# Iterated attention: the Newton step of the layer norm on GpSimd, another VectorE order, and another division of the last sums

## The reference

```python
def step(carry, _):
    q_cur, converged = carry
    scores = jnp.einsum('bhqd,bhkd->bhqk', q_cur, k) / scale
    attn = jax.nn.softmax(scores, axis=-1)
    out = jnp.einsum('bhqk,bhkd->bhqd', attn, v)
    diff = jnp.linalg.norm(out - q_cur)
    q_new = jnp.where(converged, q_cur, out)
    return ((q_new, converged | (diff < UPDATE_STEPS_EPS)), None)
(q_final, _), _ = jax.lax.scan(step, (q, jnp.asarray(False)), None, length=UPDATE_STEPS_MAX)
merged = q_final.transpose(0, 2, 1, 3).reshape(x.shape[0], x.shape[1], INNER)
return merged @ Wo + bo
```

## Time and profile before

| | before |
|---|---|
| median of 3 runs | 3225.08 us (3224.71 to 3231.12) |
| profiled execution, its own time | 3228.11 us |
| its span | 3226.8 us |
| PE busy in the span | 2926.5 us (91%) |
| DVE, ACT, POOL busy | 2524.8, 2207.4, 2008.9 us |
| mean granted clock of TensorE | 0.966 |
| iterated attention | from about 1635 us to the end |

### The profile page before, as it was taken

The page is one execution under the profiler, slowest core; times in us unless marked ns, Lnnn a source line. Parts: engine busy times, 40 slices in busy tenths (PEclk is TensorE's granted clock), DMA queues, the critical chain, the costliest instruction groups (busy, mean ns, idle before and its releaser), DMA issues.

```text
span 3226.8 us, 72034 instructions
## 1 busy us (share of the span) xinstructions
PE 2926.5 (91%) x24662; PEld 2238.6 (69%) x24663; DVE 2524.8 (78%) x5836; ACT 2207.4 (68%) x6152; POOL 2008.9 (62%) x2045
## 2 busy tenths in 40 slices
PE   5999888897799989999979999999999999999997
PEld 4666554465688868787867777777777777777775
DVE  6788887757777765564568888888888888888886
ACT  4566655653355556456448888888888888888885
POOL 2633333232455555335148888888888888888884
PEclk7999989998899989999989999999999999999998
DMA  3222422100000010201000000000000000000000
GB/s 110 74 77 77 128 78 76 52 1 7 1 1 1 1 50 24 63 1 50 14 14 2 2 2 2 2 2 2 2 2 2 2 2 2 1 2 2 1 2 27
DMA packets 68872, 77.15 MB, mean 24 GB/s; under 512 B 8017, under 2 KB 60321, under 8 KB 68385
## 3 DMA queue, kind: packets, MB, share of 16 engines
q1 hardware_dynamic: 64912, 71.10, 7.2%
q10 hardware_dynamic: 3600, 1.46, 0.2%
HBM read 52.61 MB, written 18.87 MB: 22 GB/s over the span
## 4 chain that ended last, share of the span: by engine, by line
PE 38%; DVE 9%; POOL 8%; issue 5%; ACT 4%; DVEq 0%; POOLq 0%; ACTq 0%
PE psum L2556 9%; PE psum L2538 7%; PE psum L2520 6%; POOL attn_p L3018 4%; DVE attn_pt L2817 2%; DVE sb_few L2804 2%; PE psum L1902 2%; PE psum L1753 2%; ACT attn_p L2662 2%; PE psum L1995 2%; PE psum L1755 2%; PE psum L1754 2%; PE psum L2583 2%; PE psum L1802 2%; PE psum L2462 1%
## 5 line engine op out<-in xcount | busy, mean ns | idle before, releaser
L3018 POOL TENSOR_TENSOR attn_p<-attn_p,sb_few 128x512 f32<-128x512 f32 x768 | 796.0, 1050 | 174.8 <-DVE sb_few L2811 173.5
L2662 ACT ACTIVATE attn_p<-psum,sb_few 128x256 f32<-128x256 f32 x1536 | 720.2, 479 | 61.4 <-DVE sb_few L2804 61.3
L2804 DVE TENSOR_REDUCE sb_few<-psum 128x2 f32<-128x512 f32 x768 | 507.9, 679 | 12.7 <-PE psum L2520 7.0
L2538 PE MATMUL psum<-sb_kept,attn_p 128*128 128x128 f32 x3072 | 411.4, 277 | 33.2 <-DVE attn_pt L2817 29.4
L2556 PE MATMUL psum<-attn_pt,attn_v 128*64 128x256 f32 x3072 | 384.2, 387 | 30.7 <-DVE attn_pt L2817 30.7
L502 DVE TENSOR_REDUCE sb_a_nm<-psum 128x2 f32<-128x512 f32 x512 | 329.0, 684 | 87.5 <-PE psum L392 54.1
L2538 PEld LDWEIGHTS psum<-sb_kept,attn_p 128*128 128x128 f32 x3072 | 335.4, 141 | 82.5 <-issue 30.7
L568 ACT ACTIVATE sb_a_pt<-psum 128x512 f32<-128x512 f32 x512 | 278.5, 597 | 100.4 <-PE psum L399 69.7
L2662 ACT ACTIVATION_READ_ACCUMULATOR attn_p<-psum,sb_few 128x1 f32 x1536 | 319.6, 208 | 0.0
L2556 PEld LDWEIGHTS psum<-attn_pt,attn_v 128*64 128x64 f32 x3072 | 202.7, 136 | 157.0 <-issue 75.5
L2817 DVE COPY attn_pt<-psum 128x512 f32<-128x512 f32 x384 | 263.7, 687 | 34.0 <-PE psum L2538 28.7
(11 more groups left out here) (441 smaller groups left out, 7752.1 us busy)
## 6 DMA issues: line engine op xcount, KB each, us to landing
sb_a_spread<-a_spilled SPq DMA_DIRECT2D x64, 256.0 KB, 2.9
a_spilled<-sb_a_part_hi SPq DMA_DIRECT2D x64, 128.0 KB
a_spilled<-sb_a_part_lo SPq DMA_DIRECT2D x64, 128.0 KB
sb_a_spread<-a_spilled SPq DMA_DIRECT2D x64, 128.0 KB, 2.7
sb_gate_up<-in_L_ffn_Wg SPq DMA_DIRECT2D x32, 128.0 KB
sb_gate_up<-in_L_ffn_Wu SPq DMA_DIRECT2D x32, 128.0 KB
sb_down_w<-in_L_ffn_Wd SPq DMA_DIRECT2D x32, 128.0 KB, 2.5
sb_x<-in_L_attn_x SPq DMA_DIRECT2D x4, 512.0 KB, 7.3
```

The source lines that it names most:

```text
L2538: mm = pe.transpose(PT(e)[:, kt * N + t * P:kt * N + (t + 1) * P], Pr[p % 3][:, e, t, kt * P:(kt + 1) * P], c.ident)
L2662: ins = act.activation(Pr[p % 3][:, e, t, :], S(p, e)[:, t * N:(t + 1) * N], ACT.Exp, bias=nm[:, p % 4, e, t:t + 1], accum_out=rsum[:, p % ...
L2804: dve.tensor_reduce(nm[:, p % 4, e, :], S(p, e).rearrange("p (t n) -> p t n", t=TB), AX.X, ALU.max, negate=True).then_inc(maxed.sem, 1)
L3018: pool.tensor_tensor(P3, P3, spread(rinv[:, p % 4, e, :], N), ALU.mult).then_inc(normed[e].sem, 1)
```

## The change

It does the following.

- The Newton step of every unit but the first moves from DVE to POOL, in four operations (r*r, v*that, -0.5*that+1.5, r*that), each waiting for the one before. It stands behind the first norm of rounds 3 and 4. The first unit's stays on DVE (`newton_first`).
- DVE's order: `variance(u+1, 0)` goes from the end of round 2 to behind the first maxima of round 3; `sum_squares` of q's first half to where the first Newton step was; `step_end(u, 0)` to where the second was; `step_end(u-1, 2)` to ahead of the low parts of round 3; `invert(a+1, 0)` ahead of both low parts; `add_bias(u+2, 0)` in round 5 between the two low parts.
- ACT: the second half of q's high part is made in round 5 behind the first, no longer at the start of the next unit. POOL: `differ(u, 0, 0)` goes from ahead of the first norm of round 4 to ahead of the last of round 3.
- The end: the change of step 0 is summed and its flag set in the last unit (rounds 190 and 191), that of step 1 in round 193, each with PE's sum between; the masked copies are spread over rounds 192, 193 and behind them, and the last piece of the second flag is split in 768 and 256 columns. The last two pairs of round 192 are normed and transposed in the order even, odd.
- The last sums: 8 groups of 4 tiles. ACT copies groups 0 to 3 from PSUM to SBUF and POOL adds them to x; DVE adds groups 4 to 7 from PSUM. SP stores in eight transfers of 256 KB, in the order 0, 1, 4, 2, 5, 6, 3, 7.

The diff, cut to its core:

```diff
@@ pe_program @@
             def out_product(u, s):
-                if s == 2 and u + 1 == NU:
-                    pe.wait_ge(*flagged(0))
+                if s and u + 1 == NU:
+                    pe.wait_ge(*flagged(s - 1))
...
                 if turning:
-                    turn(p + 1, 1)
-                    turn(p + 1, 0)
+                    turn(p + 1, int(r <= TURNS))
+                    turn(p + 1, int(r > TURNS))
+                if r == TURNS + 1:
+                    total(1)
...
+                if r == TURNS - 1:
+                    total(0)
...
+            for n in range(8):
+                pe.wait_ge(*chosen(4 if n == 7 else n // 2))
+                if n >= 4:
+                    pe.wait_ge(*y_copied(n - 4))
+                for m in range(4):
+                    k = 4 * n + m
+                    mm = pe.transpose(bank_of(n)[:, m * P:(m + 1) * P], xnT[:, k * P:(k + 1) * P], c.ident)
+                mm.then_inc(turned_y.sem, 1)
@@ act_program @@
                         first_high(u + 1, 0)
+                        first_high(u + 1, 1)
...
-                if i == 0 and 0 < u < NU:
-                    first_high(u, 1)
...
+                if r == TURNS + 1:
+                    square_moves(NU - 1, 1)
...
+            for n in range(4):
+                act.wait_ge(*turned_y(n))
...
+                act.copy(y_copy(n), bank_of(n)).then_inc(y_copied.sem, 1)
@@ dve_program @@
             def behind_first_maxima(u, i):
                 if i == 0 and 0 < u < NU:
                     split_q(u, 0)
+                elif i == 3 and u + 1 < NU:
+                    variance(u + 1, 0)
...
+                elif u == NU and i == 0:
+                    dve.wait_ge(*flagged(0))
+                    choose(0, 0)
+                elif i == 5 and u + 1 == NU:
+                    total(0)
...
             def behind_third_maxima(u, i):
-                if u + 1 < NU and i in (3, 4):
-                    newton(u + 1, i - 3)
+                if i == 3 and u + 1 < NU:
+                    sum_squares(u + 1, 2)
+                elif i == 4 and u < NU:
+                    step_end(u, 0)
...
+                elif r == TURNS + 1:
+                    choose(0, 1)
+                    total(1)
+                    choose(0, 2)
                 if turning:
                     move_odd(b + 1)
+                if r == TURNS + 1:
+                    flag_second()
+                    dve.wait_ge(*y_kept(STEPS * (NU - 1) + 1))
+                    c.dve_own(choose(0, 3))
+                    dve.wait_ge(*flagged(1))
+                    choose(1, 0).then_inc(chosen.sem, 1)
...
-                if turning:
-                    low(b)
+                elif i == 3 and 0 < u < NU:
+                    step_end(u - 1, 2)
                 if rising:
                     invert(a + 1, 0)
                 if turning:
+                    low(b)
+                if u + 2 < NU and i == 5:
+                    add_bias(u + 2, 0)
+                if turning:
                     low(b + 1)
...
+            choose(1, 2).then_inc(chosen.sem, 1)
+            choose(1, 3).then_inc(chosen.sem, 1)
+            step_end(NU - 1, 2)
             dve.wait_ge(*y_kept.all())
+            choose(1, 4).then_inc(chosen.sem, 1)
+            for n in range(4, 8):
+                dve.wait_ge(*turned_y(n))
+                dve.tensor_tensor(x_of(n), x_of(n), bank_of(n), ALU.add).then_inc(result.sem, 1)
@@ pool_program @@
+            def newton(u, n):
+                own = c.pool_own
+                pool.wait_ge(*rooted(2 * u + n))
+                own(pool.tensor_tensor(t_[:, :, :], rs[:, :, :], rs[:, :, :], ALU.mult))
+                own(pool.tensor_tensor(t_[:, :, :], v_[:, :, :], t_[:, :, :], ALU.mult))
+                own(pool.tensor_scalar(t_[:, :, :], t_[:, :, :], -0.5, 1.5, ALU.mult, ALU.add))
+                pool.tensor_tensor(rs[:, :, :], rs[:, :, :], t_[:, :, :], ALU.mult).then_inc(refined.sem, 1)
...
                 elif i == 4 and u < NU:
+                    if u + 1 < NU:
+                        newton(u + 1, 1)
                     differ(u, 0, 1)
...
                     elif i == 3:
+                        newton(u + 1, 0)
                         scale(u + 1, 0)
                         scale(u + 1, 1)
...
+            for n in range(4):
+                pool.wait_ge(*y_copied(n))
+                pool.tensor_tensor(x_of(n), x_of(n), y_copy(n), ALU.add).then_inc(pool_result.sem, 1)
@@ sp_program @@
-            for g in range(4):
-                nc.sync.wait_ge(*result(g))
-                store(g)
+            for n in (0, 1, 4, 2, 5, 6, 3, 7):
+                nc.sync.wait_ge(*(pool_result(n) if n < 4 else result(n - 4)))
+                store(n)
```

120 lines of the change are left out of this document (52 added, 68 removed).

## The result

| | before | after |
|---|---|---|
| median | 3224.89 us (4 runs, 3224.1 to 3231.12) | 3204.11 us (4 runs, 3202.37 to 3205.19) |
| profiled execution, its own time | 3228.11 us | 3205.19 us |
| its span | 3226.8 us | 3203.9 us |

The changed kernel takes 0.9931 of the time of before, with a 95% interval of 0.9914 to 0.9948: 20.8 us less by the medians, 22.9 us by the two profiled executions. The forecast was 3207 (3190 to 3221).

A forecast was written before the change was run, and what follows sets the result against it. TensorE's own work was taken as the bound, POOL next. 13.0 us from the repeating units plus 4.8 from the end made 17.8 off 3228.1, so 3210.3; the median lies 3.0 lower: 3207 us, range 3190 to 3221.

The forecast's parts named there:

- What bounds the kernel: TensorE's own work, 45.2 of 48.1 us a unit, is the floor; POOL is the engine next to the limit.
- Part 1: Newton off VectorE in round 4: TensorE's 0.98 us wait for the odd copy goes in 31 units, up to 30.4 us.
- Part 2: Newton on POOL, 1.24 us a step, fits its free time; the 15 units with the xnT split gain only 0.25 us.
- 16 units have 1.3 us to spare: In units without the xnT split, POOL's 1.3 us more of slack lets TensorE gain what it can.
- Rival B: Small operations on POOL meet VectorE's, about 0.56 us each; POOL becomes the bound: +23 us, 3248; chance 0.09.
- Part 3: VectorE's new order: the variance's 0.5 us is covered in round 3; the bias addition in round 5 costs 0.40 a unit.
- rival C: Only the end pays: split of q and variance meet POOL more, or Newton takes 1.7 us a step; 3220; chance 0.18.
- the steady part: The repeating units: 16 gain 0.98 - 0.40 and 15 gain 0.25, together 13.0 us less.
- Part 4: The kernel's end: stores bind, 5.5 us less, minus 0.7 for norms meeting masked copies: 4.8 us (2.5 to 6.5).
- A: Full gain: POOL keeps up in all units and the bias addition hides; 35 us less, 3190; chance 0.20.

The follow-up runs named there:

- e5: The kernel before with the new end and the Newton steps of units 1 to 31 on POOL, VectorE's order old: 3197.5 us, ratio 0.9895.
- e2: The kernel before in all of its repeating part, with only the new end: 3223.6 us, ratio 0.9976.
- e7: The changed kernel with POOL's split of xnT cut to one column for all pairs of units but the first (output differs): 3196.4 us, ratio 0.9895.
- e4: The changed kernel with the first variance back at the end of round 2: 3191.1 us, ratio 0.9873.
- e6: The changed kernel with both the first variance and the bias addition back at their old places: 3193.9 us, ratio 0.9886.
- e9: e6 with VectorE's first split of q in round 0 moved behind the second maxima, 0.6 us later: 3186.7 us, ratio 0.9873.
- e10: e4 with VectorE's first split of q in round 0 moved behind the second maxima, 0.6 us later: 3192.4 us, ratio 0.9893.
- e8: The changed kernel with four more 128x16 operations in each Newton step on POOL, same result: 3275.2 us, ratio 1.0136.
- e3: The changed kernel with the bias addition of round 5 back behind both low parts: 3199.7 us, ratio 0.9905.

## Why the prediction was right, and where its steps were not

**What bounds the kernel**: right. TensorE stayed the bound, with POOL next to it.

**Part 1**: the mechanism is right. The wait of 0.98 is gone in all units. The size was too small: with nothing else moved (e5 against e2) rounds 3 and 4 give 1.30. I had taken the idle time in brackets for the whole loss in round 4, which was 1.20, and had held that round 3's Newton step costs nothing, which was 0.10.

**Part 2**: the price is right (0.20 to 0.22 us for an operation, 1.20 a step). The estimate from the Trainium skill (GPSIMD Engine Reference, section 3.1) was 1.7 a step (redone from the same numbers, four times 1.96 x 0.16 + 0.09, it is 1.6); the trace does not agree with it for operations this small, with 0.22 us on POOL against 0.16 to 0.18 undisturbed on VectorE. I said that POOL would be 0.25 earlier and the split units gain 0.25: they gain 0.18, and e7 shows that POOL holds them. That the two numbers are so close is luck. With the first variance at its old place the split units take 47.26 to 47.28 whatever else stands where (e4, e6, e9, e10), a gain of 0.66; the variance, which I had at 0 to 0.5 there, took 0.48 of it. The step that failed is "16 units have 1.3 us to spare": e8 shows that each us more in the Newton step costs nearly one us of TensorE, in all units. Rival B would have cost more than I gave it: a step of e8 takes 2.36 us, close to B's four times 0.56, and against before its split units lose 2.1 us and the others 1.1, where I had 1.75 and 0.1.

**Part 3**: the variance is the term that was mis-sized. I had 0.5 us covered by round 3's product and POOL's queue, and gave 0.5 a unit if uncovered. It costs 0.34 in rounds 3 and 4 of every unit and 0.87 in a pair of units (e4). The path was wrong too. I looked at the product of round 3 and at POOL's queue; what is held up is VectorE's own next copy, in round 3 by the first variance itself and in round 4 by the second one, which ends with a later operation of POOL. The bias addition costs what I said, 0.37 to 0.44 in round 5. What I left out is that its delay is not a loss by itself: before, TensorE waited 0.31 us in round 0 for VectorE's end of a step, at a split of q that takes 1.80 because it meets POOL. Two delays of VectorE, one in round 5 and one in round 0, are not paid twice. The runs give all four cases for rounds 5 and 0 together, in the other units: neither delay 15.97 (e9), the long split alone 16.54 (before and e6), the bias addition alone 16.41 (after), both 16.49 (e10, a split of 1.81). So the two rounds became 0.13 shorter, where my sum had them 0.40 longer. The split of q was in my rival C as a danger; it was a cost of before that I had not looked at.

So the forecast of the steady part (13.0, measured 19.6) has three wrong terms: 0.3 too little for Newton, 0.34 too little for the variance, and 0.5 too much for rounds 5 and 0. The first two cancel in the other units; the third is the difference there (1.05 against 0.58, in 16 units). That two of them cancel is luck, and it keeps the total as near as it is.

**Part 4**: 5.1 (5.6 in e2) against 4.8, and the stores bind, as said. That it came so near is in part luck, since two errors cancel. Norms met masked copies in both rounds (3.07 for two norms above, 3.09 at 3174.86, against 2.04 undisturbed) and lost 1 us each time, where I had 0.7 in all. The last low parts came 16.5 us behind the product of the last unit's second step, against 13.8 before: 2.7 later, where I had 1.5 + 0.7. From the last low parts to the end it took 13.8 us, where I had 14.6, because I had the last product at the low clock of before (2.7 us), and it took 1.49 at a granted clock of 1.00. In e3, e5, e7 and e9, with the same end, the granted clock was 0.50 at this product; it took 2.7 us, and the way from the product of the last unit's second step to the end of the span was 31.9 to 32.2 us, not 30.3. With that clock the end would have given 3.3 to 3.5. Why the clock was granted in one run and not in another stays open: in e9 TensorE did the same work with the same waits ahead of it (1.89 and 0.66 us, in after 1.89 and 0.65).

**Rivals**: A's full gain was not reached by the change. e9, at 3186.7 (0.9873), does reach it with the variance and the bias addition where they were. C's mechanism was there in part: the variance that meets POOL costs 13 to 14 us (0.87 in each pair of units). The other part, a split of q that meets POOL more often, was not; C's time of 3220 needed both.

## What to carry over

Where two engines block each other for a whole instruction, the place of an operation matters more than its length: look in the trace for what the other engine runs at that moment, and expect the same move to pay in one version (e9, 0.57 us a unit) and not in another (e10). A wait in the profile is not its cost: what the next engine would have waited for anyway has to be taken off, and the wait of 0.36 cost nothing. Idle time of an engine over a unit is no slack; slack is what lies between the operation that grows and the first one that waits for its result. After moving work away, price its new and its old neighbours one by one: here one of two parts made the gain (29 us of span) and the other gave 10 of it back.
